# Pacing a burst of indirect fetches in a routed feed-forward layer, and pre-summing value tiles on GpSimd

## The reference, cut to what matters

```python
x = x + 0.5 * _L0_ffn_ref(_layernorm(x), Wg, W1, b1, W2, b2)
x = x + _L0_attn_ref(_layernorm(x), w_qkv, w_ky, w_proj)
x = x + 0.5 * _L0_ffn_ref(_layernorm(x), Wg, W1, b1, W2, b2)

# _L0_ffn_ref: 8 experts, 512 hidden units; each token uses only its best expert
top1_idx = argmax(softmax(x @ Wg.T)); top1_prob = its probability
y += where(top1_idx == e, (gelu(x @ W1[e].T + b1[e]) @ W2[e].T + b2[e]) * top1_prob, 0)

# _L0_attn_ref: 16 heads of 8 channels, causal (mask = lower triangle)
L   = q @ k.T * scale
agg = sum(exp(clip(q @ k_y.T * scale, -15, 15)) * mask) + EPS
r   = log(abs(L) + EPS) - log(agg + EPS)
w   = softplus(r) * mask
out = (w / (sum(w) + EPS)) @ v @ w_proj.T
```

## Time and profile before

| | |
|---|---|
| time, median of 3 runs | 454.05 us (451.23, 454.23, 454.05) |
| the profiled execution | 456.81 us, of which the span from the first to the last instruction is 455.0 us |
| busy: PE, DVE, ACT, POOL | 324.5, 310.7, 297.0, 140.0 us (71, 68, 65, 31% of the span) |
| mean granted TensorE clock | 0.805 of full speed |
| feed-forward pass 0, attention, pass 1 | roughly 0 to 97 us, 97 to 367 us, 367 to 455 us |

### The profile page before, as it was taken

The page is one execution under the profiler, slowest core; times in us unless marked ns, Lnnn a source line. Parts: engine busy times, 40 slices in busy tenths (PEclk is TensorE's granted clock), DMA queues, the critical chain, the costliest instruction groups (busy, mean ns, idle before and its releaser), DMA issues.

```text
span 455.0 us, 8174 instructions
## 1 busy us (share of the span) xinstructions
PE 324.5 (71%) x2332; PEld 200.8 (44%) x2332; DVE 310.7 (68%) x667; ACT 297.0 (65%) x862; POOL 140.0 (31%) x222
## 2 busy tenths in 40 slices
PE   6434799918577535788878598868889863359993
PEld 6424799914133211222323223233343652359993
DVE  4740344339779979999799999989897457024431
ACT  2711455622899998999899889996676471135552
POOL 5277214420044470025010250105310107710453
PEclk9998799976679755875878778698996755669998
DMA  8574255431377999003000030002100754424540
GB/s 263 190 246 131 81 138 161 130 111 66 114 197 202 217 227 180 1 1 94 0 1 2 0 94 0 2 0 68 29 0 1 226 186 139 131 85 125 168 153 23
DMA packets 37992, 47.60 MB, mean 105 GB/s; under 512 B 4288, under 2 KB 26816, under 8 KB 37696
## 3 DMA queue, kind: packets, MB, share of 16 engines
q1 hardware_dynamic: 33616, 36.20, 29.9%
q0 software_dynamic: 2560, 6.30, 4.3%
q10 hardware_dynamic: 1776, 4.60, 2.9%
HBM read 24.02 MB, written 6.29 MB: 67 GB/s over the span
## 4 chain that ended last, share of the span: by engine, by line
PE 35%; DVE 20%; ACT 17%; issue 13%; DMA 6%; SPq 3%; another core or an unknown queue 3%; POOL 1%; DVEq 0%; POOLq 0%; ACTq 0%
PE PS L1380 10%; PE PS L1390 8%; ACT R L847 7%; DVE R L1188 6%; ACT R L855 4%; PE PS L1519 3%; DVE R L1173 3%; ACT CL L847 3%; DVE CL L1173 2%; PE PS L1322 2%; DMA R<-rows_d,R 2%; SPq L449 2%; PE PS L1501 2%; PE PS L1313 2%
## 5 line engine op out<-in xcount | busy, mean ns | idle before, releaser
L1188 DVE TENSOR_TENSOR R<-PS,MB 128x1024 int32<-128x1024 int32 (+1 forms) x96 | 98.1, 1036 | 12.3 <-PE PS L1501 12.0
L742 ACT ACTIVATE R<-PS,R 128x128 f32<-128x128 f32 x184 | 52.4, 368 | 77.0 <-PE PS L1380 32.8
L855 ACT ACTIVATE R<-R 128x1024 f32<-128x1024 f32 x64 | 80.1, 1261 | 10.6 <-DVE R L1188 10.6
L847 ACT ACTIVATE R<-R 128x384 f32<-128x384 f32 (+2 forms) x192 | 77.1, 408 | 6.9 <-DVE R L1173 6.9
L1380 PE MATMUL PS<-R 128*128 (+1 forms) x368 | 56.8, 302 | 23.4 <-issue 12.6
L1486 PE MATMUL PS<-R 64*128 64x512 bf16 (+3 forms) x256 | 40.9, 373 | 31.2 <-DVE CL L1173 15.4
L1519 PE MATMUL PS<-R,V 128*32 128x256 f32 (+3 forms) x512 | 59.5, 554 | 5.1 <-ACT R L855 5.0
L1380 PEld LDWEIGHTS PS<-R 128*128 128x128 f32 x368 | 49.7, 210 | 26.4 <-issue 24.4
L1173 DVE SCALAR_TENSOR_TENSOR R<-PS,MA 128x1024 f32<-128x1024 f32 x64 | 59.7, 949 | 0.9 <-PE PS L1486 0.7
L1390 PE MATMUL PS<-R 128*128 (+1 forms) x368 | 50.7, 282 | 0.7 <-ACT R L742 0.7
L1501 PE MATMUL PS<-QPS,R 64*128 64x512 bf16 (+3 forms) x256 | 38.8, 353 | 13.8 <-DVE R L1173 8.9
(11 more groups left out here) (162 smaller groups left out, 454.9 us busy)
## 6 DMA issues: line engine op xcount, KB each, us to landing
R<-w SPq DMA_DIRECT2D x38, 258.0 KB
R<-R SPq DMA_DIRECT2D x32, 128.0 KB, 2.4
R<-R SPq DMA_DIRECT2D x16, 256.0 KB, 8.0
QPS<-R SPq DMA_DIRECT2D x32, 128.0 KB, 2.6
R<-w ACTq DMA_DIRECT2D x8, 258.0 KB
rows_d<-X SPq DMA_DIRECT2D x8, 256.0 KB, 3.8
R<-w ACTq DMA_DIRECT2D x1, 2048.0 KB, 8.5
rows_d<-R SPq DMA_DIRECT2D x8, 256.0 KB, 2.5
```

What stands on the lines that cost most here:

```text
L742: last = act.activation(HT[:, k % 2, c * P:(c + 1) * P], PS[:, k % 2, c * P:(c + 1) * P], ACT.Gelu, bias=W1[:, k, F + c:F + c + 1])
L847: act.activation(e, e, ACT.Exp, scale=SCALE, accum_out=aggf[:, ds(s + (2 * i + par) * STEPS, 1)])\
L855: act.activation(w, w, ACT.Ln, bias=1.0, scale=1.0).then_inc(s_ln, 1)
L1188: dve.tensor_tensor(weights(v)[:, :, at:at + n].bitcast(i32), PS[:, SLOTS[slot(b_fill(v, g))], 0:n].bitcast(i32), spread(mask, 1, 2), ALU. ...
```

## The change

Two edits that have nothing to do with each other.

1. `gather(r)`: from the fifth tile on (t >= AHEAD = 4), GpSimd waits before it issues the fetch of tile t until TensorE has transposed tile t-4. The wait stands in GpSimd's list, so that everything behind it (later fetches, the memset and the copies, the stores) waits too.
2. `v_prefix`: GpSimd forms the sums of the first two and the first three value tiles of the batch (`value_sums`, two operations of 128x128 into the free columns of R2), five steps ahead of the product. TensorE then multiplies ones by the first tile (128 columns) and by the two sums (256 columns) in one place, g = 1, in place of 384 columns at g = 1 and 256 + 128 at g = 2.

```diff
+AHEAD = 4
@@ build
+        VS = R2[:, HEAD_W:1536].rearrange("p (k h c) -> p k h c", k=2, h=H)
@@ gather(r)
                 for t in range(NT):
+                    if t >= AHEAD:
+                        pool.wait_ge(s_px, r * NT + t - AHEAD + 1)
                     pool.indirect_dma_start(XS[:, t, :], None, rows_d, ...)
@@ gpsimd
+            def value_sums(b):
+                if b == 0:
+                    for i in (2, 3, 8):
+                        pool.wait_ge(s_stk[i], STACK_DMAS)
+                    pool.wait_ge(s_vc, NT)
+                else:
+                    pool.wait_ge(s_cv, b)
+                of = [V[:, b * TB + i, :, 0:HD] for i in range(3)]
+                pool.tensor_tensor(VS[:, 0], of[0], of[1], ALU.add).then_inc(s_vs1, 1)
+                pool.wait_ge(s_vs1, b + 1)
+                pool.tensor_tensor(VS[:, 1], VS[:, 0], of[2], ALU.add).then_inc(s_vs, 1)
@@ for s in range(END_STEP)
+                    if at == C_AT - 5:
+                        value_sums(b)
@@ v_prefix(b, part) on TensorE
-                last = pe.matmul(PS[:, 7, shift * P:SEQ], (ones if shift else tri)[:, :],
-                                 V[:, b * TB:(b + 1) * TB - shift, :, 0:HD], start=shift == 0,
-                                 stop=shift == TB - 1)
+                    pe.matmul(PS[:, 7, :], tri[:, :], V[:, b * TB:(b + 1) * TB, :, 0:HD], start=True, stop=False)
+                else:
+                    pe.wait_ge(s_vs, b + 1)
+                    pe.matmul(PS[:, 7, P:2 * P], ones[:, :], V[:, b * TB:b * TB + 1, :, 0:HD], start=False, stop=False)
+                    pe.matmul(PS[:, 7, 2 * P:SEQ], ones[:, :], VS, start=False, stop=True).then_inc(s_cv, 1)
@@ steps
-                        for k in ((0,), (1,), (2, 3))[g]:
+                        for k in ((0,), (1,), ())[g]:
```

More of the change, by code:

```diff
@@ L338, in build @@
         s_cv = sem("v_prefix_done")
+        s_vs1 = sem("sums_of_two_value_tiles_ready")
+        s_vs = sem("sums_of_value_tiles_ready")
         s_pool = sem("pool_chain")
@@ L1534, in weighed_t, with v_prefix @@
                 last.then_inc(s_aotp, 1)
-            def v_prefix(b, shift):
-                if shift == 0:
+            def v_prefix(b, part):
+                if part == 0:
                     if b + 1 < NB:
@@ L1546, in v_prefix @@
                         pe.wait_ge(s_xnt, 2 * NB + 2)
-                last = pe.matmul(PS[:, 7, shift * P:SEQ], (ones if shift else tri)[:, :],
-                                 V[:, b * TB:(b + 1) * TB - shift, :, 0:HD], start=shift == 0,
-                                 stop=shift == TB - 1)
-                if shift == TB - 1:
-                    last.then_inc(s_cv, 1)
+                    pe.matmul(PS[:, 7, :], tri[:, :], V[:, b * TB:(b + 1) * TB, :, 0:HD], start=True, stop=False)
[3 more added lines that the diff above has]
+                    pe.matmul(PS[:, 7, 2 * P:SEQ], ones[:, :], VS, start=False, stop=True).then_inc(s_cv, 1)
             def after(s):
```

## The result

The changed kernel takes 435.36 us in the median of 4 runs (434.06 to 437.36), the kernel before beside it 454.14 us (4 runs, 451.23 to 457.11): a ratio of 0.959, 95% interval 0.9517 to 0.9663, so faster by 19 us. The profiled execution took 435.86 us (span 434.0 us), 21.0 us less than the one before.

What follows compares the result with a forecast made beforehand. It took gaps early in both passes, ending with GpSimd's fetch burst, as the bound, then TensorE. 9.8 + 12.1 + 3.3 + 0 = 25.2 us off 454.05 gave 429 us; range 421 to 444 us, own range 425 to 435.

Steps and rivals of the forecast that it cites:

- The bound: Feed-forward passes: TensorE idles early in both behind releaser-less waits, ScalarE's GELU 26.4 us and VectorE's L1062 17.7 us.
- The coincidence that pointed there: Start of both passes: waits end 1.28 and 1.25 us behind the end of GpSimd's burst of 16 fetches.
- The gaps and the half clock: Start of passes: removing the gaps gains 9.8 and 12.1 us, full clock in the slot behind them 3.3 us.
- The paced fetches: Fetches in both passes: 8.0 us for each against landings of 6.14 and 3.51 us, so no cost.
- The stores: Pass 0: first store starts 6.5 us late, delay gone after some nine stores, cost nothing; less delay in pass 1.
- The first rival: Passes: the gap comes back in part, late stores forming a burst of about nine; about 441 us, chance 0.18.
- no wait of the GELU over 3 us: Sign expected in the profile after: neither L1062 nor ScalarE's GELU waits over 3 us.
- The term 0: Attention: value sums on GpSimd gain 0 us, since VectorE sets the pace beside the removed products.
- its bounds of 3.3 and 3.7 us: Second edit: loss of 3.3 us if GpSimd's sums delay VectorE, gain of 3.7 us if TensorE's removed work counts.
- the attention as long as before, within 3 us: Sign expected in the profile after: length of the attention stage unchanged within 3 us.
- The second rival: Passes: the fetches aren't the cause of the gaps, only the second edit is left; 454 us, chance 0.12.
- Its other form: Gaps in the passes: the engines wait for their own instructions, which have DMA queues of their own; no separate chance.

Runs made afterwards that it cites:

- e1: Kernel before plus the first edit alone (fetches paced, value prefix as before): 436.81 us, ratio 0.9547.
- e4: Kernel before plus a memset of 680 columns ahead of each fetch from the fifth on, no wait on TensorE, fetches 1.8 us apart: 433.09 us, ratio 0.9474.
- e6: Kernel before with GpSimd's fetches halved to 64 KB, x rows brought unsorted by plain DMAs: 456.74 us, ratio 0.9991.
- e5: Kernel before with the 16 fetches of each pass issued by SyncE as plain DMAs of the same size, without the sort: 424.6 us, ratio 0.9292.
- e12: Kernel before, unchanged, timed and profiled once more: 453.55 us, ratio 0.9991.
- e8: Changed kernel plus a memset of 500 columns ahead of the first 12 stores of each pass: 430.81 us, ratio 0.9424 to the kernel before.
- e2: Kernel before plus the second edit alone (value sums on GpSimd, fetches unpaced): 454.76 us, ratio 0.9984.
- e10: e9 plus the value sums on GpSimd: 427.1 us, ratio 1.0 to a kernel before that took 427.02 us.
- e9: Kernel before plus 680-column memsets between fetches and 500-column memsets ahead of each pass's first twelve stores: 427.13 us, ratio 1.0003 (kernel before 427.02 us).
- e7: Kernel before plus 400-column memsets ahead of fetches from the fifth on (1.57 us apart) and the value sums on GpSimd: 435.87 us, ratio 0.9573.
- e3: Changed kernel with AHEAD = 6 and pass 0's memset and copies cut into pieces among fetches 10 to 14: 435.25 us, ratio 0.9538 to the kernel before.

## Why the prediction was right, and where it was off

**The bound** was right. The two waits with no releaser were what the passes waited for, and they went with the burst: e1 shows that pacing does it alone, e4 that distance does it without any wait, e6 and e5 that it isn't the bytes that are fetched.

**The coincidence that pointed there** was weaker than the prediction took it for; that it led to the right edit was partly luck. It set the end of VectorE's wait in pass 0 (1.28 us behind the last fetch) beside the end of ScalarE's in pass 1 (1.25 us). ScalarE's wait in pass 0 ended 48.32 - 45.54 = 2.78 us behind it, VectorE's L1062 in pass 1 started at 393.65 us, in the middle of the burst, and in e12 ScalarE came free before the last fetch was issued. So the waits end near the end of the burst, but not at one distance from it. The evidence is in e1, e4 and e8, which change when GpSimd issues its DMAs and leave the passes' other work as it is.

**The gaps and the half clock**, 9.8 + 12.1 + 3.3 = 25.2 us: the front of the passes gained 12.1 + 14.0 = 26.1 us, slot 2 at full clock included (1.96 and 1.94 us against 3.54 and 3.78). These terms were good to 1 us.

**The paced fetches** cost nothing, as predicted. The waits over the span have TensorE waiting for a fetch twice, 10.9 us in all, once for the first fetch of each pass.

**The stores are the step that failed.** The prediction had the last fetch, memset and copies end at about 60.3 us and the first store start 6.5 us late; they ended at 59.5 us, and the first store started at 59.67 us. It then wrote "Cost: nothing". That held for the stores' own times and overlooked what the same text had just found: that GpSimd's DMAs 1.3 us apart are what stops the other engines. The first rival did say it ("a burst of about nine") and was dismissed with "a gap among them stops the burst at once". It takes five stores in pass 0 and a fetch and three stores in pass 1 until that gap is there, and each costs its idle time and a half clock behind it: 8.6 us between the profiles, and e8 gets 6.9 of them back. By the prediction's own sign, no wait of the GELU over 3 us, the one of 3.08 us at 63.90 us was a miss too. Had this term been in the sum, it would have given 454.05 - 25.2 + 8.6 = 437.5 us, against 435.36 measured. The outcome lies at the upper end of the forecast's own range (425 to 435), half-way to the first rival's 441, with that rival's mechanism; it is inside the range of 421 to 444.

**The second edit** was taken at nothing, because VectorE sets the pace beside the removed products. The profiles before and after seemed to contradict this with 3.6 us. e2, e10 and e12 decide: 0.9984 alone, 0.03 us between e9 and e10, and 281.49 against 286.13 us in two executions of the kernel before. The term 0 was right, its bounds of 3.3 and 3.7 us were generous, and "the attention as long as before, within 3 us" was a bad test, since the same program misses it.

**The second rival**, that fetches aren't the cause, falls where the gaps occur. Its other form, that the engines wait for their own instructions, falls too: the profile has no packet of the two instruction queues from 34 to 57 us in the kernel before, and none from 57 to 72 us in the changed one, so no such transfer ended the gaps there. The Trainium skill's page "SBUF — State Buffer", section "SBUF: two separate sides", which among the engines lets only VectorE and GpSimd hold each other up, isn't contradicted in what it speaks of, accesses of SBUF: halving the bytes changed nothing (e6), and the same bytes fetched by SyncE held nobody (e5). But it doesn't follow from it that ScalarE can't be held by GpSimd's DMA work. In the earlier trace rows and in e6's row it was, for 12.6 and 12.7 us.

**What stays open.** What in the chip holds the signals back, whether it takes GpSimd, the indirect kind or both, and what made the kernel before 27 us faster in one series. Most rows fit a backlog that grows when indirect DMAs come nearer than one each 1.6 to 1.8 us (e7 and e4) and that must be worked off before what TensorE signals gets through. Its rate could differ where something outside differs. Against it speaks that four or five close ones were enough behind fetches 2 us apart, where no backlog should have been left, and seven from rest were not. This is argued, not shown: no run measured the backlog, and the one series in which the gap seems to have been absent has no profile of a burst. Whether the change is worth anything under that condition wasn't tried either; e9's 1.0003 suggests not.

**The best version** depends on the same thing. Of those with the sort, e8 is the fastest measured where the gaps occur (430.81 us, ratio 0.9424 against 0.959 of the change, with intervals that don't overlap; from e4's 0.9474 it can't be told apart). e9 should be at least as good there and leaves out the wait on TensorE, but ran only beside a kernel before that had nothing to lose.

## What to carry to other kernels

When a burst is found to hurt, ask at once what the cure delays and whether that will come as a burst of its own: here spacing the fetches pushed the stores into one, and a third of the gain went back. A wait whose releaser the profile can't name is worth a table of what else ends near it, for every engine and every place where it occurs, and then an experiment that moves only the suspect. And before a difference in a stage is put down to an edit, profile the old kernel twice and compare the granted clock: a step of 6.0 and of 8.5 us was one program at two clocks.

## What the runs showed of the hardware

- Where the effect occurred, VectorE and ScalarE went on late after TensorE had finished, beside indirect DMAs issued by GpSimd 1.25 us apart. Seven in a row from rest gave no wait over 2 us (e3, pass 0), behind eight VectorE waited 4.1 us (e3, pass 1, where the first transposes also come sooner), beside sixteen ScalarE waited 10.7 to 15.4 us and VectorE 10.5 to 11.8 us in pass 0, in two shorter waits in pass 1. Behind fetches at a steady 2 us, four or five sufficed, behind fetches at 1.8 us one fetch and two stores (e4, pass 1: 2.9 us).
- The waits ended near the end of the burst, at no fixed distance. VectorE's in pass 0 ended 1.28 (before) and 1.11 us (e12) after the end of the last fetch and 0.1 us ahead of it in e6; ScalarE's in pass 0 ended 2.8 us after it in before and e6; ScalarE's in pass 1 ended 1.25 us after it in before and 1.6 us ahead of it in e12.
- At 1.57 us apart a slot lost some 1 us now and then, at 1.8 us nothing while the fetches lasted. The size, 64 or 128 KB, made no difference; the same bytes in plain DMAs of SyncE, in a denser burst, gave no gap.
- It wasn't always so, it seems: one series of five had the kernel before at 427.0 us and not at 454 to 457.
- The attention took 286.1 us in one execution of the kernel before and 281.5 us in another. 2.5 us of the 4.6 lie in step 19, which took 8.5 us at a granted clock of 0.74 and 6.0 us at 1.00.
